# A softmax attention on one core: row maxima in steps of eight tiles, scores 14 tiles behind, outputs gathered by SBUF transfers instead of transposes

## The chip, the cores and the metric

The kernel runs on one core of a Trainium2 chip. The metric is the device time of one execution in microseconds (us), the median over runs. Engines in the text: PE (TensorE), DVE (VectorE), ACT (ScalarE), POOL (GpSimd), and SP (SyncE), which here only issues transfers.

## The reference

The program is four layers on 2 x 1024 tokens of width 128: a delta-rule attention, a mixture of experts (two of eight), a softmax attention with rotary positions, and a second mixture of experts (one of eight). Only the third layer changes:

```python
x = layernorm(h)
q, k, v = x @ Wq.T + bq, x @ Wk.T + bk, x @ Wv.T + bv     # 16 heads of 8, 2 sequences of 1024
q, k = rope(q), rope(k)
p = softmax(q @ k.T / sqrt(8))                              # 1024 x 1024 for each head and sequence
h = h + (p @ v) @ Wo.T + bo                                 # then the layernorm of the next layer
```

## The kernel before

**Precision by rows.** A head has only 8 dimensions, so q and k are split into three bf16 parts and the products of parts are laid on 56 rows (`KR`) of the contraction. The parts are stored to DRAM by `store`, and loaded again in that layout by `load`, `load_q` and `group`. There are two copies: one on partitions 64 to 119 (`S1B`), for the maxima, and one on partitions 0 to 58 (`KA`), whose three extra rows carry the negated row maximum in three bf16 parts, so that the second product already is the score minus its maximum.

**Stages.** Four heads of one sequence make a group; there are eight (`G`). The work on them is one long pipeline:

- A *tile* is 128 queries of one head against all 1024 keys: two matmuls of 512 columns (`max_half`) into a pair of PSUM banks, and one DVE `tensor_reduce` (`max_tile`, L1063) to a column of maxima. There are 256 tiles, and two pairs of banks take turns.
- After every 16 tiles (512 queries of four heads), POOL negates and splits the 16 columns (`split_rows`), PE turns them into rows (`turn_rows`, L950), ACT copies the rows to SBUF (`rows`, L1192), and SP sends them to the extra rows of q (`max_rows`, L1347). A counter `e` numbers these rounds.
- A *unit* is one block of 128 keys against 512 queries for four heads: four score matmuls (`scores`, L961) into banks that rotate by three, four exponentials of 128x512 on ACT (L1201), and four fp32 matmuls with the values (`values`, L974), two units later, which add up in bank 7. There are 128 units, and eight of them complete 512 queries. A column of ones beside the values gives the sum of the exponentials. ACT copies bank 7 to `a1_o` (L1214).
- PE's order is written out by hand: 22 tiles (`AHEAD`) first, then in each unit two tiles and the four scores, half and half, with the values of two units before. The last 11 units have no tiles beside them. The first unit of each eight waits for the row transfer (`a1_mrow`).

**After the last tile** DVE takes the 16 outputs one by one (`turn`): a 32x32-block transpose of 128x512 (L1086), a reciprocal of the sums (L1090) and a product (L1091), and after each four a transpose back (`turn_back`, L1096). PE then multiplies by Wo (`project_out`, L983); the first two of these four stand in PE's order inside the last units. DVE adds the result to x (`add_out`, L1101) and takes the statistics of the next layernorm (L118, L121).

**SP's order** is also written out by hand. Its queue first stores q and k, then loads groups as buffers come free. In the first rounds loads, stores and row transfers alternate; from round 3 on, every second round also issues the two loads of a later group.

Of the kernel before, what the change touches and what calls it, by code (L numbers as in the profile page):

```python
# [12 lines left out]
P = 128  # L13
# [10 lines left out]
AHEAD_AT = TABLES_AT - 12376 - 3076  # L24
# [775 lines left out]
AHEAD = 22  # L800
# [6 lines left out]
OUT_UNITS = {G * U - 7: 0, G * U - 5: 1}  # L807
# [5 lines left out]
def evictions():  # L813


    out = [("rows", 0)]
    for n in range(G * U * HG):
        out.append(("score", n))
        if n % HG == 1 and n // HG % NTB == NTB - 2 and n // HG + 2 < G * U:
            out.append(("rows", (n // HG + 2) // NTB))  # L820
    return out
# [16 lines left out]
def attn1_memory(c, w):  # L838
    c.sb("a1_part", [P, 4, 3, BLK], BF16)
    c.sb("a1_v", [P, NT, D])  # L840
    c.sb("a1_q", [P, NG, QH, HG, BLK], BF16)
# [3 lines left out]
    c.sb("a1_mx", [P, 2, HG * 4])  # L845
    c.sb("a1_mn", [P, 2, HG * 4])
    c.sb("a1_mt", [P, P], BF16)
    c.sb("a1_ob", [P, 2, BLK])
    c.sb("a1_rd", [P, 2, BLK // 32])
# [3 lines left out]
def attn1_ahead(c):  # L853

    pool, at = c.pool, AHEAD_AT
    for name, shape, dtype in (("a1_k", [P, NG, HG, L], BF16), ("a1_va", [P, NTB, NH, 32], F32), ("a1_ms", [P, 3, HG * 4], BF16), ("a1_id", [P, P], BF16)):
        c.mem[name] = c.arena.cut(at, shape, dtype)
        at += words_of(shape, dtype)
# [3 lines left out]
    pool_step(c, pool.memset(c.mem["a1_va"][:, :, :, HD:HD + 1], 1.0))  # L862
# [3 lines left out]
def attn1_loads(c, w):  # L866

    at = TABLES_AT - 3076
    c.ahead = Count(c.nc, "ahead")
    for name, shape, whole in (("wq", [D, D], False), ("wqs", [D, D], False), ("wk", [D, D], False), ("wks", [D, D], False),  # L870
                               ("wv", [D, D], False), ("wo", [D, D], False), ("bcol", [D, 4], False), ("bv", [P, D], True),
                               ("bo", [P, D], True), ("cos", [D, L], False), ("sin", [D, L], False)):
# [7 lines left out]
def tile_at(n):  # L880

    return n // 32, n % 32 // 16, n % 16 // 4, n % 4
# [7 lines left out]
def attn1_pe(c):  # L890
# [25 lines left out]
    def max_half(n, half):  # L916
        g, qh, h, qt = tile_at(n)
        k, bank = g % NG, 3 + 2 * (n % 2)
        if half == 0:
# [5 lines left out]
            if n == 16:  # L925
                pe.wait_ge(S("a1_second"), 16)
            if n >= 32 and n % 32 == 0:
                pe.wait_ge(S(f"a1_one{g}"), 3 * 16)
# [3 lines left out]
        mm = pe.matmul(ps[:, bank + half, :], q[rows, k, qh, h, qt * P:(qt + 1) * P],  # L932
# [10 lines left out]
    def turn_rows(e):  # L943
# [6 lines left out]
        pe.matmul(ps[0:3 * HG * 4, bank_of(i), 0:P], m["a1_ms"][:].rearrange("p i a -> p (i a)"), m["a1_id"][:],  # L950
                  start=True, stop=True).then_inc(S("a1_s2"), 1)

    def scores(u, h):
        st, qh, kb = u // U, u % U // NTB, u % NTB
        k, i = st % NG, TAKEN["score", u * HG + h]
        if h == 0 and u % U == 0:
            pe.wait_ge(S(f"a1_two{st}"), 3 * 16)
        if h == 0 and kb == 0:
            pe.wait_ge(S(f"a1_mrow{qh}"), 16 * (st + 1))
# [4 lines left out]
    def values(u, half=None):  # L964
        st, qh, kb = u // U, u % U // NTB, u % NTB
        at = slice(0, BLK) if half is None else slice(half * (BLK // 2), (half + 1) * (BLK // 2))
        if half != 1:
            if kb == 0:
                pe.wait_ge(S("a1_va"), st + 1)
                if u >= NTB:  # L970
                    pe.wait_ge(S("a1_o"), u // NTB)
            pe.wait_ge(S("a1_exp"), TAKEN["score", u * HG + HG - 1] + 1)
        for h in range(HG):
            mm = pe.matmul(ps[32 * h:32 * h + 32, 7, at], va[:, kb, (st % NG) * HG + h, :],  # L974
                           pt[:, (u % 3) * HG + h, at], start=kb == 0 and half != 1, stop=kb == NTB - 1, skip_group_check=True)
        if half != 0:
            mm.then_inc(S("a1_pv"), 1)

    def project_out(b):
        pe.wait_ge(S("a1_back"), b + 1)  # L980
        pe.wait_ge(S("a1_exp"), max((i + 1 for i in range(FIVE, len(TAKEN)) if bank_of(i) == 3 + b), default=1))
        for j in range(TPB):
# [1662 lines left out]
```

## Time and profile before

| | |
|---|---|
| median of 3 runs | 858.94 us (858.55 to 862.6) |
| profiled execution | 860.77 us, of which the span is 859.0 us |
| TensorE's granted clock, mean over the span | 0.903 |
| busy over the whole span | PE 715.8, DVE 658.8, ACT 526.6, POOL 238.3 us |
| the changed layer | about 399 to 762 us of the span |

Times in the views are microseconds from the span's start; "x" counts instructions. A name after an arrow in brackets is what an idle engine waited for. `arena` is the one big SBUF allocation, so most tiles have this name. SPq rows are transfers being issued.

### The profile page before, as it was taken

The page shows a single profiled execution, that of the slowest core. Times are in us where ns is not written, and L with a number is a line of the kernel's source. Part 1 is how long each engine was busy: PE and PEld are TensorE (multiplying, and loading weights), DVE is VectorE, ACT ScalarE, POOL GpSimd, SP SyncE. Part 2 cuts the span into 40 slices and gives each one's busy share as a digit, 9 for nine tenths or more (in the row PEclk, how much of TensorE's full clock was granted, in tenths as well). Part 3 has the DMA queues.
Part 4 walks back from the last instruction along what each step waited for, and adds up shares of the span by engine and source line. Part 5 has one row for each costly group of instructions (what it writes and reads, how often), then busy time and mean ns, then how long its engine had stood idle before and what let it go on. Part 6 is the DMA issues. An engine that isn't in the chain of part 4 may idle for free. (4 is left out here: it accounts for less than half of the span.)

```text
span 859.0 us, 20505 instructions
## 1 busy us (share of the span) xinstructions
PE 715.8 (83%) x8024; PEld 359.3 (42%) x8024; DVE 658.8 (77%) x1317; ACT 526.6 (61%) x1028; POOL 238.3 (28%) x295
## 2 busy tenths in 40 slices
PE   5999978887736999963989999999999999946880
PEld 2333236553426999961412222222222222236770
DVE  7887985446875555537799999999999999664555
ACT  3763622365713444425629999999999999624453
POOL 0130010204216767552473300100000100006773
PEclk9999989997856999985958999999999999767995
DMA  3440010000082311221756650403300000032123
GB/s 101 98 100 3 1 24 5 4 3 1 0 302 95 110 48 50 38 61 60 205 129 148 170 126 2 88 16 75 73 16 2 2 2 9 4 128 84 50 50 101
DMA packets 40968, 55.47 MB, mean 65 GB/s; under 512 B 9210, under 2 KB 31234, under 8 KB 40490
## 3 DMA queue, kind: packets, MB, share of 16 engines
q1 hardware_dynamic: 36906, 46.04, 20.1%
q0 software_dynamic: 3968, 8.13, 3.5%
q8 instruction: 64, 1.05, 0.5%
q14 instruction: 30, 0.25, 0.1%
HBM read 35.22 MB, written 14.55 MB: 58 GB/s over the span
## 5 line engine op out<-in xcount | busy, mean ns | idle before, releaser
L1063 DVE TENSOR_REDUCE arena<-psum 128x1 f32<-128x1024 f32 x256 | 292.8, 1217 | 10.4 <-PE psum L932 10.4
L1201 ACT ACTIVATE arena<-psum 128x512 f32<-128x512 f32 x512 | 276.5, 597 | 18.7 <-PE psum L961 11.4
L932 PE MATMUL psum<-arena 56*128 56x512 bf16 x512 | 164.5, 404 | 4.7 <-DVE arena L1063 3.6
L974 PE MATMUL psum<-arena 128*32 128x256 f32 (+1 forms) x1944 | 163.4, 408 | 5.9 <-issue 5.9
L961 PE MATMUL psum<-arena 59*128 59x512 bf16 x512 | 158.4, 390 | 0.1
L369 PE MATMUL psum<-arena 128*128 128x128 f32 x808 | 108.1, 281 | 0.4 <-DVE arena L420 0.4
L369 PEld LDWEIGHTS psum<-arena 128*128 128x128 f32 x808 | 102.0, 198 | 0.7 <-DVE arena L420 0.7
L974 PEld LDWEIGHTS psum<-arena 128*32 128x32 f32 x1944 | 38.8, 108 | 107.5 <-issue 61.6
L932 PEld LDWEIGHTS psum<-arena 56*128 56x128 bf16 x512 | 28.9, 95 | 115.6 <-DVE arena L1063 97.9
L485 POOL DMA_INDIRECT rows_y<-arena x62 | 62.6, 1009 | 37.7 <-DVE arena L434 31.9
L396 PE MATMUL psum<-arena 128*128 (+1 forms) x496 | 66.5, 277 | 2.8 <-ACT arena L464 2.0
L480 POOL DMA_INDIRECT arena<-rows_x,arena x62 | 60.0, 968 | 26.0 <-issue 17.4
L1273 POOL TENSOR_SCALAR arena<-arena 128x16 f32<-128x16 f32 x16 | 4.1, 254 | 220.4 <-DVE arena L1063 220.3
L396 PEld LDWEIGHTS psum<-arena 128*128 128x128 f32 x496 | 60.3, 192 | 4.8 <-issue 3.3
L461 ACT ACTIVATE arena<-psum 128x512 f32<-128x512 f32 x39 | 23.3, 597 | 44.1 <-PE psum L369 44.1
L453 ACT COPY arena<-arena 128x512 f32 x39 | 24.1, 618 | 32.0 <-PE psum L369 19.4
L2300 PE MATMUL psum<-arena 128*32 128x512 f32 x352 | 41.2, 593 | 0.2 <-DMA arena<-arena 0.2
L424 DVE TENSOR_TENSOR arena<-arena,psum 128x512 f32<-128x512 f32 x39 | 26.8, 687 | 18.4 <-PE psum L369 18.4
L961 PEld LDWEIGHTS psum<-arena 59*128 59x128 bf16 x512 | 30.6, 94 | 17.3 <-ACT arena L1201 14.2
L434 DVE COPY arena<-psum 128x128 f32<-128x128 f32 x62 | 18.1, 292 | 25.0 <-PE psum L396 13.5
L2040 ACT ACTIVATE arena<-psum 128x64 f32<-128x64 f32 x32 | 7.2, 225 | 44.7 <-PE psum L2322 44.7
L417 DVE COPY arena<-arena 128x512 f32 x39 | 17.0, 437 | 19.2 <-issue 16.2
(314 smaller groups left out, 1059.5 us busy)
## 6 DMA issues: line engine op xcount, KB each, us to landing
arena<-scr_q SPq DMA_DIRECT2D x32, 224.0 KB
arena<-scr_k SPq DMA_DIRECT2D x15, 448.0 KB
arena<-in_f_up SPq DMA_DIRECT2D x1, 4096.0 KB, 14.0
arena<-rows_y SPq DMA_DIRECT2D x12, 256.0 KB, 4.8
scr_q<-arena SPq DMA_DIRECT2D x6, 384.0 KB, 5.3
arena<-in_f_down SPq DMA_DIRECT2D x1, 2048.0 KB, 17.0
arena<-in_f_up SPq DMA_DIRECT2D x1, 2048.0 KB, 9.4
rows_x<-xn SPq DMA_DIRECT2D x5, 256.0 KB, 13.0
```

Of the source, the lines that this page charges most:

```text
L369: mm = pe.matmul(ps[:, bank, f * P:(f + 1) * P], w[:, a.pair, at], xt[:, a.pair, :], start=True, stop=True)
L396: mm = pe.matmul(ps[:, 5 + 2 * d.pair, 0:P], h[:, d.pair, f * P:(f + 1) * P], merged(wdown[:, ed, f * P:(f + 1) * P]), start=f == 0, stop= ...
L424: dve.tensor_tensor(h[:, u.pair, :], sg[:, u.pair, :], ps[:, 2 + u.pair, :], ALU.mult).then_inc(hidden, 1)
L453: act.copy(m["e_w"][:, x0.pair, F:2 * F], merged(m["e_up"][:, bass.ds(e, 1), F:2 * F])).then_inc(picked2, 1)
L480: pool.indirect_dma_start(xs[:, t % GATHERED, :], None, src, index).then_inc(landed[t % GATHERED], 16)
L485: pool.indirect_dma_start(dst, index, y[:, d.slot, :], None).then_inc(stored[d.slot], 16)
L932: mm = pe.matmul(ps[:, bank + half, :], q[rows, k, qh, h, qt * P:(qt + 1) * P], kk[rows, k, h, half * BLK:(half + 1) * BLK], start=True, s ...
L961: pe.matmul(ps[:, bank_of(i), :], kk[0:KA, k, h, kb * P:(kb + 1) * P], q[0:KA, k, qh, h, :], start=True, stop=True).then_inc(S("a1_s2"), 1)
L974: mm = pe.matmul(ps[32 * h:32 * h + 32, 7, at], va[:, kb, (st % NG) * HG + h, :], pt[:, (u % 3) * HG + h, at], start=kb == 0 and half != 1 ...
L1063: dve.tensor_reduce(mx[:, qh, h * 4 + qt:h * 4 + qt + 1], ps[:, bank:bank + 2, :].rearrange("p a b -> p (a b)"), X, ALU.max).then_inc(S("a ...
L1201: act.activation(pt[:, (u % 3) * HG + h, :], ps[:, bank_of(i), :], ACT.Exp, scale=float(HD) ** -0.5).then_inc(S("a1_exp"), 1)
L2300: mm = pe.matmul(ps[32 * h:32 * h + 32, fir_bank(n, i), :], m["a0_wfir"][:, (g0 + g) * H0 + h, :], v4[:, h, b, PAD + t0 - 4 * g:PAD + t0 - ...
```

## The change

- The row maxima go on in rounds of 8 tiles (`TE`), that is 256 queries (`QW`) of four heads. There are 32 rounds (`QE`) of split, turn, copy and row transfer in place of 16.
- PE runs 14 tiles ahead of the scores, not 22. The last 7 units have no tiles beside them.
- A unit is two key blocks against 256 queries. Its four score banks each hold two heads, so a score of 512 columns becomes two matmuls of 256. The values add up in the first half of bank 7, over four units, and ACT's copy of the output is 128x256, 32 times. The loads of q are cut into four of 256 queries.
- The ones beside the values fill eight columns, so that each head's sum of exponentials comes out on eight rows. SP gathers the rows of each output into one dense array in `xnT`, and the replicated sums into `xn`: eight transfers of 8 rows x 256 for each of 30 outputs (`collect`). The last two outputs are gathered by two small matmuls with a 0/1 matrix (`pick`).
- DVE's 16 transposes, reciprocals and products and its four transposes back are gone. In their place there are reciprocals of 128x256 and products of 128x256 (`divide`, `divide_last`).

The core of the diff (from layout, memory and loads only the lines that the text speaks of):

```diff
-AHEAD = 22
+QW, TE, UE = 256, 8, 4
+QE = TILES // TE
+AHEAD = 14
-OUT_UNITS = {G * U - 7: 0, G * U - 5: 1}
+OUT_UNITS = {G * U - 6: 0, G * U - 5: 1, G * U - 3: 2}
...
         free_bank(i)
-        pe.matmul(ps[:, bank_of(i), :], kk[0:KA, k, h, kb * P:(kb + 1) * P],
-                  q[0:KA, k, qh, h, :], start=True, stop=True).then_inc(S("a1_s2"), 1)
+        for x in range(2):
+            h = 2 * (j % 2) + x
+            mm = pe.matmul(ps[:, bank_of(i), x * QW:(x + 1) * QW], kk[0:KA, k, h, kb * P:(kb + 1) * P],
+                           q[0:KA, k, e % 4, h, :], start=True, stop=True)
+        mm.then_inc(S("a1_s2"), 1)
...
+    def divide(n):
+        at = slice(n * QW, (n + 1) * QW)
+        of = slice(0, P if n < 6 else 96)
+        dve.wait_ge(S(f"a1_dense{n}"), (NG if n < 6 else NG - 1) * 2 * HG * 16)
+        dve_step(c, dve.reciprocal(sums[of, at], sums[of, at]))
+        z = dve.tensor_tensor(dense[of, at], dense[of, at], sums[of, at], ALU.mult)
...
-    for n in range(2 * NG):
-        turn(n)
-    turn_back(0)
-    turn_back(1)
...
+    for n in range(4):
+        divide(n)
+    add_out(0)
+    add_out(1)
+    divide(4)
+    divide(5)
     add_out(2)
...
+    def collect(e):
+        g, n = e // 4 % NG, e // 16 * 4 + e % 4
+        at = slice(n * QW, (n + 1) * QW)
+        part = o[:, e // 2, e % 2 * QW:(e % 2 + 1) * QW]
+        sp.wait_ge(S("a1_o"), e + 1)
+        for h in range(HG):
+            to = slice((g * HG + h) * HD, (g * HG + h + 1) * HD)
+            sp.dma_start(dense[to, at], part[32 * h:32 * h + HD, :]).then_inc(S(f"a1_dense{n}"), 16)
+            sp.dma_start(sums[to, at], part[32 * h + HD:32 * h + 2 * HD, :]).then_inc(S(f"a1_dense{n}"), 16)
...
     group(0, 0, "a1_two0")
     group(S1B, 1, "a1_one1")
+    store_all(4)
     max_rows(0)
...
+    for e in (5, 6):
+        max_rows(e)
+    for e in range(4):
+        collect(e)
     store_all(7)
-    for e in range(3, 2 * G):
+    for e in range(7, QE):
+        collect(e - 3)
         max_rows(e)
-        if e % 2 == 1 and e // 2 + 3 < G:
-            g = e // 2 + 3
+        if e % 4 == 3 and e // 4 + 3 < G:
+            g = e // 4 + 3
```

How rows of the program move, at three places. First SP, where the first maxima are sent. Before, from the load of the second half of the first q on; the rows named scr_q and scr_k are loads or stores of q and k, and L1347 is the row transfer of round 0:

```order
L1332 DMA arena<-scr_q 56x4x512
L1332 DMA arena<-scr_k 56x4x1024
L1332 DMA arena<-scr_q 56x4x512 x2
L1332 DMA arena<-scr_k 56x4x1024
L1332 DMA arena<-scr_q 56x4x512 x2
L1347 DMA arena<-arena 3x16x128
```

After the change, at the same place (L1349 is the load, L1342 the store, L1363 the row transfer):

```order
L1349 DMA arena<-scr_q 56x4x256 x2
L1349 DMA arena<-scr_k 56x4x1024
L1349 DMA arena<-scr_q 56x4x256 x4
L1349 DMA arena<-scr_k 56x4x1024
L1349 DMA arena<-scr_q 56x4x256 x4
L1342 DMA scr_k<-arena 128x3x512
L1342 DMA scr_k<-arena 128x2x512 x2
L1363 DMA arena<-arena 3x8x128
```

Ahead of the first row transfer there now stand twelve loads in place of seven, and three stores that stood behind it.

Second SP, ahead of the row transfer of round 7 of the changed kernel. It is preceded by the transfers of rounds 5 and 6 (one row, "x2"), then 32 gathering transfers (16 times the pair L1372, L1373), and then:

```order
L1342 DMA scr_q<-arena 128x3x512 x2
L1342 DMA scr_q<-arena 128x512
L1372 DMA xnT<-arena 8x256
L1373 DMA xn<-arena 8x256
L1372 DMA xnT<-arena 8x256
L1373 DMA xn<-arena 8x256
L1372 DMA xnT<-arena 8x256
L1373 DMA xn<-arena 8x256
L1372 DMA xnT<-arena 8x256
L1373 DMA xn<-arena 8x256
L1363 DMA arena<-arena 3x8x128
```

Before, between one row transfer and the next, SP had at this depth of the program (from round 2 to round 3):

```order
L1347 DMA arena<-arena 3x16x128
L1332 DMA arena<-scr_k 56x4x1024
L1332 DMA arena<-scr_q 56x4x512 x2
L1325 DMA scr_q<-arena 128x3x512 x2
L1325 DMA scr_q<-arena 128x512
L1325 DMA scr_q<-arena 128x3x512 x2
L1325 DMA scr_q<-arena 128x512
L1347 DMA arena<-arena 3x16x128
```

So 43 transfers stand between the row transfers of rounds 6 and 7, where no more than nine stood between two of them before.

Third DVE, behind the last `tensor_reduce`. Before, from the tiles to the first of the 16 outputs:

```order
L1063 TENSOR_REDUCE arena<-psum 128x1 x256
L1086 STREAM_TRANSPOSE arena<-arena 128x512
L1090 RECIPROCAL arena<-arena 128x16
L1091 TENSOR_TENSOR xn<-arena 128x16x8
L1086 STREAM_TRANSPOSE arena<-arena 128x512
```

After the change:

```order
L1101 RECIPROCAL xn<-xn 128x256
L1102 TENSOR_TENSOR xnT<-xnT,xn 128x256
L1115 TENSOR_TENSOR x<-x,psum 128x512
L118 BN_STATS bn<-x 128x6 x4
L121 BN_AGGR mv<-bn 128x2 x4
L1115 TENSOR_TENSOR x<-x,psum 128x512
```

The reciprocal is now of 256 elements on each partition, where it was of 16, and it comes ten times in all (four of them in a row before the first `add_out`), where it came 16 times.

## Rows read from the trace of the kernel before

**Rows 1.** The page, busy time of each engine over the span

```profile
PE 715.8 (83%) x8024; PEld 359.3 (42%) x8024; DVE 658.8 (77%) x1317; ACT 526.6 (61%) x1028; POOL 238.3 (28%) x295
```

**Rows 2.** Busy time by stretch: engines, granted clock, share of the DMA engines, GB/s

```profile
428.00:442.00 14.00, 12.31 (x24) 1.49 (x24) 14.00 (x13) 2.47 (x4) 10.15 (x11) 0.50 0.69 148
...
446.00:461.00 15.00, 13.96 (x92) 2.94 (x90) 14.22 (x13) 11.46 (x23) 4.85 (x5) 0.66 0.77 185
461.00:465.00 4.00, 4.00 (x45) 1.10 (x41) 4.00 (x4) 3.94 (x9) 2.41 (x7) 1.00 0.01 2
560.00:590.00 30.00, 29.24 (x317) 7.29 (x313) 29.62 (x27) 29.18 (x57) 1.09 (x5) 1.00 0.32 63
732.80:743.00 10.20, 10.20 (x40) 2.91 (x37) 9.68 (x30) 5.08 (x10) 0.00 (x0) 0.50 0.00 0
```

**Rows 3.** Timeline: start, length, instruction, idle before; rounds of 16 tiles, exponentials alone

```profile
702.11 0.25 POOL L1273 TENSOR_SCALAR arena<-arena 128x16 f32<-128x16 f32 x1 [17.02 <-DVE arena L1063]
704.71 0.25 ACT L1192 CAST arena<-psum 48x128 bf16<-48x128 f32 x1
712.70 0.59 ACT L1214 COPY arena<-psum 128x512 f32<-128x512 f32 x1
720.51 0.25 POOL L1273 TENSOR_SCALAR arena<-arena 128x16 f32<-128x16 f32 x1 [17.02 <-DVE arena L1063]
744.44 6.48 ACT L1201 ACTIVATE arena<-psum 128x512 f32<-128x512 f32 x13
```

**Rows 4.** Timeline of the start: first tiles, loads of two groups, first score

```profile
423.18 22.37 DVE L1063 TENSOR_REDUCE arena<-psum 128x1 f32<-128x1024 f32 x19 [6.01 <-PE psum L932]
428.69 0.35 SPq L1332 DMA_DIRECT2D arena<-scr_k  x1
448.54 0.58 PE L961 MATMUL psum<-arena 59*128 59x512 bf16 x1
449.05 2.36 SPq L1325 DMA_DIRECT2D scr_k<-arena  x3
```

**Rows 5.** SP's issues by line: duration ns min/median/max, first and last start

```profile
L1332 SPq DMA_DIRECT2D arena<-scr_q x32: 307/419/2028, 417.3 to 616.9; - x32
L1347 SPq DMA_DIRECT2D arena<-arena x16: 697/716/863, 445.3 to 723.7; - x16
L1576 SPq DMA_DIRECT2D arena<-arena x32: 507/592/894, 29.9 to 52.2; - x32
```

**Rows 6.** Timeline and stretches: a row transfer waited for; loads of two groups

```profile
723.66 0.70 SPq L1347 DMA_DIRECT2D arena<-arena  x1
725.84 0.11 PEld L961 LDWEIGHTS psum<-arena 59*128 59x128 bf16 x2 [0.61 <-DMA arena<-arena]
540.07 0.46 SPq L1332 DMA_DIRECT2D arena<-scr_k  x1
552.00:554.00 2.00, 2.00 (x26) 0.54 (x24) 2.00 (x3) 1.96 (x5) 0.00 (x0) 1.00 0.04 8
```

**Rows 7.** DVE's groups by shape over the span: busy, mean ns

```profile
L1775 DVE TENSOR_TENSOR xn<-arena 128x256 f32<-128x256 f32 x4 | 1.6, 428 | 0.0
...
L1858 DVE RECIPROCAL arena<-arena 128x32 f32<-128x32 f32 x2 | 0.7, 354 | 0.1
L1090 DVE RECIPROCAL arena<-arena 128x16 f32<-128x16 f32 x16 | 4.1, 254 | 0.6
```

**Rows 8.** Timeline of the end: a wait of PE, the add and statistics, next layer

```profile
731.05 1.16 PE L983 MATMUL psum<-arena,xnT 128*128 128x128 f32 x8 [1.11 <-DVE xnT L1096]
752.23 0.69 DVE L1101 TENSOR_TENSOR x<-x,psum 128x512 f32<-128x512 f32 x1 [7.46 <-PE psum L983]
752.95 0.87 DVE L118 BATCH_NORM_STATS2 bn<-x 128x6 f32<-128x128 f32 x4
753.86 0.38 DVE L121 BATCH_NORM_AGGREGATE mv<-bn 128x2 f32<-128x6 f32 x4
761.75 0.19 DVE L668 TENSOR_SCALAR rs<-mv 128x4 f32<-128x4 f32 x1 [1.26 <-PEq L2621]
```

More of the change, by code:

```diff
@@ L818, in evictions @@
         out.append(("score", n))
-        if n % HG == 1 and n // HG % NTB == NTB - 2 and n // HG + 2 < G * U:
-            out.append(("rows", (n // HG + 2) // NTB))
+        if n % HG == 1 and n // HG % UE == UE - 2 and n // HG + 2 < G * U:
+            out.append(("rows", (n // HG + 2) // UE))
     return out
@@ L931, in max_half @@
         rows = slice(S1B, S1B + KR)
-        mm = pe.matmul(ps[:, bank + half, :], q[rows, k, qh, h, qt * P:(qt + 1) * P],
+        mm = pe.matmul(ps[:, bank + half, :], q[rows, k, qq, h, qt * P:(qt + 1) * P],
                        kk[rows, k, h, half * BLK:(half + 1) * BLK], start=True, stop=True)
@@ L964, in values, with scores @@
[L964 to L972, printed above, removed]
+    def scores(u, j):
+        st, e, kb = u // U, u // UE, 2 * (u % UE) + j // 2
+        k, i = st % NG, TAKEN["score", u * HG + j]
+        if j == 0 and u % U == 0:
+            pe.wait_ge(S(f"a1_two{st}"), 5 * 16)
+        if j == 0 and u % UE == 0:
+            pe.wait_ge(S(f"a1_mrow{e % 2}"), 16 * (e // 2 + 1))
+        free_bank(i)
+        for x in range(2):
[3 more added lines that the diff above has]
+        mm.then_inc(S("a1_s2"), 1)
@@ L973, in values @@
+    def values(u, i):
+        st, e, kb = u // U, u // UE, 2 * (u % UE) + i
+        if kb == 0:
+            pe.wait_ge(S("a1_va"), st + 1)
+            if e:
+                pe.wait_ge(S("a1_o"), e)
+        pe.wait_ge(S("a1_exp"), TAKEN["score", u * HG + 2 * i + 1] + 1)
         for h in range(HG):
-            mm = pe.matmul(ps[32 * h:32 * h + 32, 7, at], va[:, kb, (st % NG) * HG + h, :],
-                           pt[:, (u % 3) * HG + h, at], start=kb == 0 and half != 1, stop=kb == NTB - 1, skip_group_check=True)
@@ L987, in attn1_pe, with project_out @@
+    def project_out(b, halves=range(2)):
+        if b >= 2:
+            pe.wait_ge(S("a1_added"), b - 1)
+        for n in halves:
+            pe.wait_ge(S("a1_back"), 2 * b + n + 1)
+            for j in (2 * n, 2 * n + 1):
+                mm = pe.matmul(ps[:, 3 + b % 2, j * D:(j + 1) * D], xnT[:, (b * TPB + j) * P:(b * TPB + j + 1) * P],
+                               m["a1_wo"][:], start=True, stop=True)
+        if halves[-1] == 1:
+            mm.then_inc(S("a1_out"), 1)
     project(0)
@@ L1117, in attn1_dve @@
     dve.tensor_scalar(rs[:, most], mv[:, most, 1], 1e-5, None, ALU.add).then_inc(S("a1_nvar"), 1)
-    turn(halves - 1)
-    turn_back(3)
+    divide(6)
+    divide(7)
     dve.wait_ge(S("a1_nroot"), 1)
@@ L1182, in attn1_act @@
     biased(7)
-    for n in (4, 5):
-        leading(n)
-        following(n)
+    leading(4)
+    following(4)
     def rows(e):
@@ L1418, in attn1_layout @@
     out["a1_wv"] = a["L1_attn_Wv"].T
-    out["a1_wo"] = a["L1_attn_Wo"].T.reshape(NG, HG, HD, D).transpose(1, 0, 2, 3).reshape(D, D)
+    out["a1_wo"] = a["L1_attn_Wo"].T
+    pick = np.zeros((HG, 32, 2, HG, HD), np.float32)
+    for h in range(HG):
+        for d in range(HD):
+            pick[h, d, 0, h, d] = pick[h, HD, 1, h, d] = 1
+    out["a1_sel"] = pick.reshape(P, 64)
     bq, bk = a["L1_attn_bq"], a["L1_attn_bk"]
```

217 lines of the change are left out of this document (106 added, 111 removed).

## The prediction

> **What bounds the kernel now.** I read the page first: no engine is busy all the time, since the program is four layers [rows 1]. Only the third changes, so I went on by stretches. From 560 to 590 us, in the middle of the pipeline, DVE is busy 29.62 of 30 us and reduces 27 tiles, one in 1.107 us; ACT is busy 29.18 us [rows 2]. DVE sets the pace, and ACT is close behind. The timeline gives the round: the same POOL instruction comes at 702.11 and at 720.51 [rows 3], 18.40 us for 16 tiles. That is 1.150 us a tile and 2.30 us a unit. 16 x 1.107 would be 17.71, so 0.69 us a round is lost around the row copy of 0.25 us and the output copy of 0.59 us on ACT [rows 3]. Exponentials alone go at 6.48 / 13 = 0.50 us each, a unit at 2.0 us [rows 3].
>
> The start: tiles begin at 423.18 us and go at 22.37 / 19 = 1.177 us each, at half the clock [rows 2, 4]; the first score starts at 448.54, after 22 tiles [rows 4]. The end: the last tile is reduced by 720.4 (this is when POOL starts its last round, and the outputs begin), and the next layer starts at 761.75 [rows 8]. So the tail behind the last tile is 41.4 us. In it PE waits 1.11 us for DVE at 731.05 [rows 8], and from 732.8 to 743 it runs at the lower clock, 0.50 [rows 2].
>
> The total is thus the start of the tiles, plus 256 tiles at DVE's pace, plus every stall of DVE among them, plus the tail. Running 14 tiles ahead and not 22 doesn't shorten the row of 256 tiles; it leaves 7 units behind it and not 11, which pays only if the tail was bound by these units.
>
> **The first score (+6.5, bounds 0 and +8.5).** With 14 tiles ahead DVE runs dry at 423.2 + 14 x 1.177 = 439.7 unless the scores have begun. They wait for the row transfer of round 0. Before, it had an empty queue. Now twelve loads and three stores stand ahead of it. Three sets of this size (two groups of loads, one set of stores) were issued from 446 us on, the stores last, at 449.05 [rows 4], and the DMA engines were done by 461, at most 15 us after [rows 2]. From 428.7, when the first load is issued [rows 4], that gives about 443.5; the q loads, cut in pieces half as long, may add 1. The row transfer lands right behind, about 445.5, and DVE goes on at 446.2: a stall of 6.5 us. Low bound: small transfers get past the big ones. Then SP's issues alone count: 12 x 0.46, three stores 2.4, the transfer's own 2.16 us from issue to landing (723.66 to 725.82, where the weight load at 725.84 waited for it [rows 6]). That is before 439.7, and costs nothing. High bound: the loads slow each other by 2 us more.
>
> **The 43 transfers ahead of round 7 (+11, bounds +6 and +19).** A round now is 4 units, 9.2 us. The row copy falls in the middle of the third unit, and the scores that need the transfer come 1.5 units (3.45 us) behind the turn on PE, which with the copy of 0.25 us on ACT [rows 3] and the hand-over takes 0.5: about 3.0 us behind SP's start. So between two row transfers SP has 9.2 us, and 0.8 of slack (3.0 less 2.16). Between rounds 6 and 7 it must issue 40 gathering transfers and three stores. What one costs: loads 0.42 at the median and 0.31 at least; transfers from SBUF to SBUF 0.59 with 32 rows, 0.70 with the row transfer [rows 5]; 0.04 us lie between two. For 8 rows I take 0.40 + 0.04, near the loads, since it has fewer rows than either SBUF transfer. 40 x 0.44 = 17.6, the stores 2.4, the row transfer's own issue 0.7: 20.7, against 10.0 allowed. Stall 10.7. With 0.31 + 0.02 it is 6, with 0.59 + 0.04 it is 18.5. PE executes in order, so the tiles queued behind that score wait too, DVE has at most two tiles in its banks, and ACT nothing.
>
> The Trainium skill, "DMA: Bandwidth & Descriptors", section "Anatomy of one DMA — SWDGE (gpsimd) path", puts the sequencer's dispatch at about 50 ns. At that price 40 transfers would be 2 us, and this stall would not exist; the rows of SP's queue show six to fourteen times as much, and the sum goes by them.
>
> **Rounds with group loads (+6, bounds 0 and +12).** Four rounds (7, 11, 15, 19) issue ten loads behind the row transfer, and then eight gathering transfers stand ahead of the next one. Issue: 0.7 + 10 x 0.46 + about 0.8 for one slow one (the maximum is 2.0 [rows 5]) + 3.5 = 9.6 us, just over 9.2. Worse, the data: two groups issued from 540.07 keep the DMA engines busy until 552 [rows 6], 12 us; with half-length pieces 12.5 to 13. A row transfer issued at +9.6 lands behind them at about +13.7, and it is due at 9.2 + 3.0 = 12.2. That is 1.5 us a round, four rounds. Low bound: nothing, if it overtakes. High bound: 3 us each. Before, 18.4 us lay between two row transfers, so this was hidden.
>
> **Clock (+3, bounds 0 and +8).** Behind the 1.11 us wait at 731.05 the granted clock was at its lower level (1.2 GHz of 2.4) for 10.2 us, and ACT did 10 exponentials in them [rows 2], 1.0 us each and not 0.5. A stall of 11 us will do the same. I take 2 us for the long one and 1 for the others; part of the low stretch lies in the stalls.
>
> **Per round (+3.5, bounds 0 and +11).** The losses of 0.69 come from one row copy and one output copy. Now there are two of each in the same time, with the output copy half as wide (about 0.35). I take 0.9 in place of 0.69, 16 times. If the loss does not shrink with the copy it is 16 x 0.69 = 11. ACT stays under DVE: 16 x 0.50 + 0.25 + 0.35 = 8.6 against 8 x 1.107 = 8.86 us.
>
> **The tail (-5.5, bounds -19 and 0).** DVE's reciprocals: 16 elements 254 ns, 32 elements 354 ns [rows 7]. That is 6.25 ns an element, so 256 elements take 1.75 us. With the product of 0.43 [rows 7] and the gap a `divide` is 2.25 us. An `add_out` is 0.69 + 0.87 + 0.38 [rows 8] and gaps, 2.05. From the last tile: four divides 9.0, two add_outs 13.1, two divides 17.6; PE waits for these two before it projects (0.7) and `add_out(2)` ends at 20.5. Two divides of 96 partitions 25.0 (time goes by elements on a partition), small ones 25.6, `divide_last` 27.8, four rows of norm 29.0, `divide_last` 31.2, PE 0.7, the last `add_out` 34.0, and 1.3 to the next layer (the gap ahead of 761.75 [rows 8]): 35.3. With 0.6 for waits, 35.9 against 41.4. PE and ACT need only 7 units (14 us) and three projections in this time, so DVE is the bound. If a reciprocal took one cycle an element (0.43 us, like the product), ten would be 13.2 shorter and PE the bound: about 22.5 us, -19. The other end is 0: waits of PE and the lower clock eat the gain.
>
> The Trainium skill, "VectorE: DVE Perf Modes", section "First, the fixed hardware budget", says that a reciprocal iterates with a repeat count of 8. With the page's 0.96 GHz that is an estimate of 2.1 us for 256 elements, and the tail would be 3.8 us longer than by the rows.
>
> **At nothing:** POOL's split (five instructions, under 1.5 us, due 2.2 us later as before), the wider memset (hidden in the layer before), the table loads of the next layer (SP has them out long before 35 us of tail have passed).
>
> **Sum:** 6.5 + 11 + 6 + 3 + 3.5 - 5.5 = +24.5 us, on the profiled execution's 860.8: 885.3. That execution is 1.8 above the median of the runs, so I predict 883.
>
> **Rivals.**
> - *Only the long stall.* Row transfers overtake the group loads, so the rounds with loads cost nothing, and the first score comes on time: 858.9 + 11 + 2 + 3.5 - 5.5 = 870. For it: no row shows a small transfer behind a big one. Against: the loads of one queue finish one after the other. 18 in 100.
> - *Short reciprocals.* The tail takes -19 in place of -5.5: 870. Against: the two shapes above give a slope of six cycles. 10 in 100.
> - *Weight loads bind PE.* Each score now takes two weight loads where it took one, and the values in the tail twice as many. In the steady stretch PE is modelled busy 29.24 of 30 us [rows 2]. If 0.06 us of each of the 512 extra loads shows, +30 more: 910. Against: DVE's reduce, not PE, is back to back, and most of a load hides behind the matmul before. 7 in 100.
> - *SP's queue is never late* (the other side). If a gathering transfer issues in at most (10.0 - 0.7 - 2.4) / 40 = 0.17 us and small transfers land past big ones, all waits are gone, the clock stays up, and the tail gain is kept: 858.9 + 3.5 - 5.5 = 857, and 853 if the rounds lose nothing more. It decides at 0.17 us; no issue of these lines is under 0.307 [rows 5]. 7 in 100. The dispatch figure of the Trainium skill named above is the rule by which it would come out this way.
> - The forecast: 58 in 100, its own range 871 to 900.
>
> **From the cases to the numbers.** About 0.5% is what a measurement here can tell from no change, 4.3 us. The queue rival splits: 4 faster, 3 the same. Some of the 870 cases, with a start at its low bound, end within 0.5%: 3. So faster 0.05, the same 0.06, slower 0.89. To leave out no more than 2 in 10, the range runs from 865 to 905: the bottom takes in the two cases of 870, the top the long issue (0.63 each, +8) with the high bound of the load rounds.
>
> **What would show each step.** SP's issues of the gathering lines at about 0.4 us; PE's score waiting some 11 us for the row transfer at about 510 us of the span, with a gap in DVE's reduces; shorter waits 9 us later and then each 37 us, three times; the first score at about 445 with DVE idle before it; reciprocals of 128x256 at 1.75 us; about 36 us from the last reduce to the next layer. The prediction is wrong if SP's issues are below 0.2 us, if row transfers land 2.2 us after issue while group loads run, or if PE's period with split scores is above DVE's.

## The result and the profile after

The changed kernel takes 903.49 us (median of 4 runs, 899.7 to 904.37) against 858.75 us before (856.66 to 862.6), a ratio of 1.0507 with a 95% interval of 1.0459 to 1.0555. That is 44.7 us more, where 24.5 were forecast: inside the range of 865 to 905 us, in the direction, and too little by nearly half. The profiled execution took 903.59 us, its span 902.3.

The page of the changed kernel: busy time of each engine, and two of its costliest groups (busy, mean ns | idle just before them and what ended it):

```profile
PE 728.8 (81%) x8664; PEld 411.3 (46%) x8664; DVE 663.7 (74%) x1285; ACT 528.1 (59%) x1061; POOL 253.1 (28%) x375
...
L1082 DVE TENSOR_REDUCE arena<-psum 128x1 f32<-128x1024 f32 x256 | 298.0, 1217 | 48.7 <-PE psum L932 46.6
...
L963 PE MATMUL psum<-arena 59*128 59x256 bf16 x1024 | 168.4, 283 | 31.2 <-DMA arena<-arena 23.5
```

DVE's busy sum moves by 4.9 us [rows 1], so the loss isn't work. The reduces sat idle for 48.7 us, and PE's scores waited 23.5 of theirs for a row transfer. Where the idle time lies is read from the timeline of the reduces (start, length, count, idle before):

```profile
422.39 16.49 DVE L1082 TENSOR_REDUCE arena<-psum 128x1 f32<-128x1024 f32 x14 [6.01 <-PE psum L932]
443.64 5.99 DVE L1082 TENSOR_REDUCE arena<-psum 128x1 f32<-128x1024 f32 x5 [4.76 <-PE psum L932]
...
488.79 22.32 DVE L1082 TENSOR_REDUCE arena<-psum 128x1 f32<-128x1024 f32 x19 [0.24 <-PE psum L932]
530.27 1.23 DVE L1082 TENSOR_REDUCE arena<-psum 128x1 f32<-128x1024 f32 x1 [19.16 <-PE psum L932]
532.63 1.22 DVE L1082 TENSOR_REDUCE arena<-psum 128x1 f32<-128x1024 f32 x1 [1.14 <-PE psum L932]
534.39 7.12 DVE L1082 TENSOR_REDUCE arena<-psum 128x1 f32<-128x1024 f32 x6 [0.53 <-PE psum L932]
542.93 2.51 DVE L1082 TENSOR_REDUCE arena<-psum 128x1 f32<-128x1024 f32 x2 [1.42 <-PE psum L932]
...
583.70 2.51 DVE L1082 TENSOR_REDUCE arena<-psum 128x1 f32<-128x1024 f32 x2 [1.82 <-PE psum L932]
...
625.16 1.22 DVE L1082 TENSOR_REDUCE arena<-psum 128x1 f32<-128x1024 f32 x1 [2.60 <-PE psum L932]
...
666.21 1.22 DVE L1082 TENSOR_REDUCE arena<-psum 128x1 f32<-128x1024 f32 x1 [2.08 <-PE psum L932]
...
669.90 93.26 DVE L1082 TENSOR_REDUCE arena<-psum 128x1 f32<-128x1024 f32 x80 [0.82 <-PE psum L932]
```

The first gap is behind exactly 14 tiles. The big one, 19.16 us, is at round 7. Then come four groups of gaps about 41 us apart, each with two or three small gaps behind the first. These lie in stretches of the lower clock: the granted clock is 0.51 from 585 to 588 us, and 0.50 from 668 to 670. The last 80 tiles run without a gap. In SP's queue ahead of the big gap (first and last rows of the 43 transfers):

```profile
498.00 0.70 SPq L1363 DMA_DIRECT2D arena<-arena  x1
498.75 0.71 SPq L1372 DMA_DIRECT2D xnT<-arena  x1
...
519.93 0.62 SPq L1373 DMA_DIRECT2D xn<-arena  x1
520.60 1.56 SPq L1342 DMA_DIRECT2D scr_q<-arena  x3
522.21 0.67 SPq L1372 DMA_DIRECT2D xnT<-arena  x1
...
527.59 0.77 SPq L1363 DMA_DIRECT2D arena<-arena  x1
...
538.59 0.77 SPq L1363 DMA_DIRECT2D arena<-arena  x1
```

From the row transfer of round 6 to that of round 7 SP needs 29.6 us. Forty gathers take 0.667 each, 26.7 us, three stores 1.6. And PE's first score of round 7 starts 2.0 us behind the issue:

```profile
529.59 0.39 PE L963 MATMUL psum<-arena 59*128 59x256 bf16 x1 [18.87 <-DMA arena<-arena]
```

By stretch (PE, weight loads, DVE, ACT and POOL busy, granted clock, DMA share, GB/s), the big gap, what follows it, the steady part and the tail:

```profile
512.00:529.00 17.00, 0.00 (x0) 0.00 (x0) 0.00 (x0) 0.00 (x0) 0.00 (x0) 0.54 0.20 65
529.00:540.00 11.00, 10.24 (x104) 3.97 (x104) 8.00 (x7) 7.82 (x16) 1.01 (x5) 0.78 0.91 173
...
700.00:760.00 60.00, 58.83 (x732) 23.87 (x729) 59.62 (x53) 57.76 (x118) 6.49 (x31) 1.00 0.04 10
763.00:806.00 43.00, 31.68 (x249) 15.73 (x248) 30.50 (x65) 22.41 (x46) 1.11 (x6) 0.81 0.08 26
```

In the big gap no engine works, and the DMA engines are busy a fifth of the time: the kernel waits for SP to issue, not for bandwidth. The tail takes from the last reduce (763.16) to 805.94, 42.8 us. DVE in it:

```profile
763.08 1.74 DVE L1101 RECIPROCAL xn<-xn 128x256 f32<-128x256 f32 x1
764.86 0.42 DVE L1102 TENSOR_TENSOR xnT<-xnT,xn 128x256 f32<-128x256 f32 x1
...
781.00 0.69 DVE L1115 TENSOR_TENSOR x<-x,psum 128x512 f32<-128x512 f32 x1 [1.31 <-PE psum L998]
...
794.06 0.23 DVE L1133 RECIPROCAL rs<-rs 128x12 f32<-128x12 f32 x1 [6.62 <-ACT rs L1230]
...
799.97 1.76 DVE L1109 RECIPROCAL xn<-psum 32x256 f32<-32x256 f32 x1 [2.08 <-PE psum L989]
...
805.94 0.19 DVE L668 TENSOR_SCALAR rs<-mv 128x4 f32<-128x4 f32 x1 [0.87 <-PEq L2662]
```

The divides cost what was forecast, but DVE waits 6.62 us for a root on ACT. ACT takes it behind the last exponentials, and these are late because PE, which goes through its list in order, first stood before the third projection:

```profile
779.74 1.22 PE L998 MATMUL psum<-arena,xnT 128*128 128x128 f32 x4 [1.35 <-DVE xnT L1102]
780.89 1.03 PE L963 MATMUL psum<-arena 59*128 59x256 bf16 x4
```

Its next scores take 1.03 us and no longer 0.61: the granted clock is 0.50 from 780 to 789. Between the last exponentials, which end at 788.5, and the root ACT has two things more, and both are part of DVE's wait: the copy of the last output, which waits 3.50 us for PE's last products with the values, and the load of the table for the root.

```profile
792.04 0.37 ACT L1208 COPY arena<-psum 128x256 f32<-128x256 f32 x1 [3.50 <-PE psum L975]
792.43 1.28 ACT L165 ACT_TABLE_LOAD   x1
...
793.83 0.20 ACT L1230 ACTIVATE rs<-rs 128x12 f32<-128x12 f32 x1
```

Where the 43.3 us between the spans are (859.0 and 902.3), against the forecast's own terms.

| | forecast | measured | from |
|---|---|---|---|
| start | 6.5 | 4.4 | gaps of the reduces to round 6, 6.7 us, less 2.3 before |
| ahead of round 7 | 11, and 2 of clock | 20.8 | gaps of the reduces, 19.16 + 1.14 + 0.53 |
| rounds with group loads | 6, and 1 of clock | 13.1 | their gaps: 2.7, 3.1, 4.0, 3.3 |
| pace, rest | 3.5 | 5.3 | 340.8 us from first to last tile, less 297.2 before, less the three rows above |
| tail | -5.5 | +1.4 | 42.8 less 41.4 |

The other layers add -0.8 and -0.9 us, which no run explains.

### The profile page after: what moved, and what is told of

Same layout as the page of the kernel before. It is cut to its first block and busy times, and to the rows that moved or that the text cites. A ratio compares the mean times of both kernels' runs of the same rounds, so it can differ in the third digit from the quotient of the medians.

```text
span 902.3 us, 22268 instructions
## 1 busy us (share of the span) xinstructions
PE 728.8 (81%) x8664; PEld 411.3 (46%) x8664; DVE 663.7 (74%) x1285; ACT 528.1 (59%) x1061; POOL 253.1 (28%) x375
## 5 line engine op out<-in xcount | busy, mean ns | idle before, releaser
L1082 DVE TENSOR_REDUCE arena<-psum 128x1 f32<-128x1024 f32 x256 | 298.0, 1217 | 48.7 <-PE psum L932 46.6
L963 PE MATMUL psum<-arena 59*128 59x256 bf16 x1024 | 168.4, 283 | 31.2 <-DMA arena<-arena 23.5
L975 PE MATMUL psum<-arena 128*32 128x256 f32 x2048 | 170.9, 406 | 5.1 <-issue 5.1
L963 PEld LDWEIGHTS psum<-arena 59*128 59x128 bf16 x1024 | 76.2, 96 | 56.9 <-DMA arena<-arena 19.2
L1284 POOL TENSOR_SCALAR arena<-arena 128x8 f32<-128x8 f32 x32 | 7.4, 232 | 248.4 <-DVE arena L1082 242.0
L975 PEld LDWEIGHTS psum<-arena 128*32 128x32 f32 x2048 | 42.6, 110 | 63.7 <-ACT arena L1217 34.8
L2081 ACT ACTIVATE arena<-psum 128x64 f32<-128x64 f32 x32 | 7.2, 225 | 42.2 <-PE psum L2363 42.1
```

What stands on the lines that cost most here:

```text
L963: mm = pe.matmul(ps[:, bank_of(i), x * QW:(x + 1) * QW], kk[0:KA, k, h, kb * P:(kb + 1) * P], q[0:KA, k, e % 4, h, :], start=True, stop=True)
L975: mm = pe.matmul(ps[32 * h:32 * h + 32, 7, 0:QW], va[:, kb, (st % NG) * HG + h, :], pt[:, (u % 3) * HG + 2 * i + h // 2, h % 2 * QW:(h % 2 ...
L1082: dve.tensor_reduce(mx[:, e % 4, n % TE:n % TE + 1], ps[:, bank:bank + 2, :].rearrange("p a b -> p (a b)"), X, ALU.max).then_inc(S("a1_red ...
```

## The experiments

The twelve runs below were made on three chips. The kernel before takes 886.79 us on the first (spread, none, the rounds with group loads, the start), 855.16 on the second (the changed kernel again, pairs, the third projection, the four edits together) and 858.34 on the third (22 tiles ahead, no reciprocals, gathers of four rounds, divides on POOL). So runs on different chips are compared by their ratio to the kernel before, and microseconds are subtracted only on one chip or between traces. The changed kernel itself was measured in the result above and on the second chip; for the other two its ratio is taken to be the same, 1.0507 to 1.0535. The changed kernel on the second chip:

**The changed kernel again.** 

> The changed kernel as it is, as the reference of the other runs on the same chip. Both theories: the ratio to the kernel before stays near 1.05 (1.043 to 1.057), whatever the chip's own level, and the long gap of DVE ahead of round 7's scores is 19 us again.

900.65 us, ratio 1.0535 (1.0498 to 1.0572); the long gap is 19.17 us, and the tail 42.2 us (the last reduce ends at 761.08, the next layer starts at 803.31). The interval overlaps that of the result, so no effect of the chip on the lost share can be told.

### The 240 gathering transfers

**Spread.**
```diff
+    later = [(e, heads) for e in range(QE - 2) for heads in ((0, 1), (2, 3))]
     for e in range(7, QE):
-        collect(e - 3)
         max_rows(e)
...
+        for _ in range(1 if e % 4 == 3 and e < 20 else 3):
+            if later and later[0][0] <= e - 2:
+                collect(*later.pop(0))
```


> Edit: the same 240 gathering transfers, but each row transfer is issued first and the gathers are spread behind it, six to twelve... at most twelve a round (four behind a round that loads groups), so that SP's issues fit into a round. Queue theory (SP's issue time of 0.67 us for each of 40 gathers is the 19 us stall ahead of round 7): that stall goes, with the half-clock units behind it, 20 us less, 884 us; the waits in the rounds with group loads stay if they are the data's, and shrink by up to 1 us each if they are SP's. Rival (the stall is the landing of stores and gathers in the DMA engines, not their issue): the same bytes flow in the same stretch, so the stall would move behind another round and the time stay above 895.

Ratio 1.0193 (1.0116 to 1.027), 3.1 to 3.4 points of the ratio, some 27 to 29 us, under the changed kernel. The same 240 transfers, none ahead of round 7. That is more than the 20 us expected: the long gap is gone and has moved nowhere else, and the gaps of the load rounds shrink from 13.1 to 5.8 us in all, since the row transfer is now ahead of the gathers. Reduces from the middle of round 4 on:

```profile
503.99 31.61 DVE L1082 TENSOR_REDUCE arena<-psum 128x1 f32<-128x1024 f32 x27 [0.24 <-PE psum L932]
537.12 37.46 DVE L1082 TENSOR_REDUCE arena<-psum 128x1 f32<-128x1024 f32 x32 [1.53 <-PE psum L932]
575.79 37.46 DVE L1082 TENSOR_REDUCE arena<-psum 128x1 f32<-128x1024 f32 x32 [1.21 <-PE psum L932]
```

**None.** `collect` issues nothing, and the divides wait for the outputs alone.


> Leaves out all 240 gathering transfers (the output is not the attention's). Prices them all. Queue theory: the long stall is gone and SP is free in every round; what stays are the waits behind the data of two groups. 882 us, within 3 us of the kernel with spread gathers. If gathers also cost elsewhere (SBUF ports, DMA engines), it is more than 5 us below that kernel.

Ratio 1.014 (1.0067 to 1.0213), 4.2 us under the spread version on the same chip. Reduces from the middle of round 4 on:

```profile
502.89 69.18 DVE L1082 TENSOR_REDUCE arena<-psum 128x1 f32<-128x1024 f32 x59 [0.24 <-PE psum L932]
572.52 37.46 DVE L1082 TENSOR_REDUCE arena<-psum 128x1 f32<-128x1024 f32 x32 [0.45 <-PE psum L932]
610.84 37.46 DVE L1082 TENSOR_REDUCE arena<-psum 128x1 f32<-128x1024 f32 x32 [0.86 <-PE psum L932]
648.47 95.44 DVE L1082 TENSOR_REDUCE arena<-psum 128x1 f32<-128x1024 f32 x82 [0.18 <-PE psum L932]
```

At the first load round no gap is left that makes a row of its own, and at the others 0.45, 0.86 and 0.18 us: with the gathers away, ten loads are hardly felt. I had expected the waits behind the loads' data to stay. All gathers together cost 32 to 34 us (3.7 to 4.0 points), of which their order alone gives back 27 to 29.

**Pairs.** One transfer for two rounds (the divides wait for it):
```diff
-        part = o[:, e // 2, e % 2 * QW:(e % 2 + 1) * QW]
+        if e % 2 == 0:
+            return
+        n, at = n - 1, slice((n - 1) * QW, (n + 1) * QW)
+        part = o[:, e // 2, :]
```


> The gathering transfers carry two rounds at once, 8 rows of 512 columns, so 120 of them take the place of 240 and move the same bytes. Theory A (a transfer holds SP's queue for a time of its own, 0.62 us, whatever its size): 20 transfers of 13.3 us with gaps stand ahead of round 7 in place of 26.7, the long gap of DVE falls from 19.2 us to about 6, and the kernel is 12 to 16 us faster than the changed one. Theory B (issue time goes by bytes): each issues in 1.1 us or more, the gap stays at 17 to 21 us and the time is within 3 us.

886.45 us, ratio 1.0381 (1.0329 to 1.0433), 14.2 us under the changed kernel on the same chip. SP's issues of it, with twice the bytes each (line: duration ns min/median/max, first and last start):

```profile
L1374 SPq DMA_DIRECT2D xnT<-arena x60: 624/624/712, 499.5 to 755.8; - x60
```

The changed kernel's own row has the same minimum and a median one nanosecond longer:

```profile
L1372 SPq DMA_DIRECT2D xnT<-arena x120: 624/625/878, 498.8 to 771.2; - x120
```

The bytes have no part in the price. The long gap falls to 3.12 us:

```profile
515.03 1.23 DVE L1082 TENSOR_REDUCE arena<-psum 128x1 f32<-128x1024 f32 x1 [3.12 <-PE psum L932]
```

My 6 counted 20 transfers; it is 16, since the fifth round has no partner yet: 16 x 0.667 + 1.6 + 0.7 = 13.0 us, less the 10.0 that the forecast allowed, is 3.0.

### The rounds with group loads

```diff
             group(S1B, g, f"a1_one{g}")
-            sp.wait_ge(S("a1_pv"), U * (g - NG + 1))
-            group(0, g, f"a1_two{g}")
+        if e % 4 == 1 and 8 < e < 22:
+            g = e // 4 + 2
+            sp.wait_ge(S("a1_pv"), U * (g - NG + 1))
+            group(0, g, f"a1_two{g}")
```


> Edit: of the two group loads that four rounds issue together, the second is issued two rounds later. The waits behind them were 13 us in all in the changed kernel (DVE idle in rounds 8, 12, 16, 20 with the half clock after it). Data theory (the row transfer lands behind 1.8 MB of loads): with half of it ahead, 5 us of data against 9.2 us of round, all four go: 903.5 - 13 = 890 or 891. Rival (SP's issue is late by itself, 0.8 + 5.3 + 5.3 us of issues against 9.2): with five loads fewer it also fits, but round 7's neighbour, round 8, stays late, since SP is still behind there: 894. A third view, that small transfers pass big ones, gives no change.

Ratio 1.0381 (1.0306 to 1.0455), 1.3 points or 11 us under the 1.0507 of the changed kernel, with intervals that just don't meet. Past round 7 the timeline has one row for 184 tiles:

```profile
550.30 213.69 DVE L1082 TENSOR_REDUCE arena<-psum 128x1 f32<-128x1024 f32 x184 [0.60 <-PE psum L932]
```

All four waits are gone, and only they. With this run and the one without gathers, neither the loads nor the gathers alone make these waits: both stand between two row transfers. In the changed kernel the row transfer behind the first such round was issued at 538.59, 11.0 us after the one before (9.6 forecast), and the first score behind it started at 542.5, 3.9 us later and not 2.0. In the other three such rounds the row transfer comes 11.5 to 11.9 us after the one before, and the score 2.9 to 3.4 us behind it. So it is issued late and it also lands late.

### The start

```diff
     group(0, 0, "a1_two0")
-    group(S1B, 1, "a1_one1")
-    store_all(4)
     max_rows(0)
+    group(S1B, 1, "a1_one1")
+    store_all(4)
```


> Edit: the row transfer of round 0 is issued ahead of the second group's loads and the three stores. DVE stood idle 4.8 us behind tile 14 and 1.4 us soon after. Theory (the first row transfer lands behind loads and stores): it lands at about 438, before DVE is through with 14 tiles; 903.5 - 6 = 897.5. Rival (the first group's own data is what the first score waits for, not the rows): that lands only 2 us earlier, 901 or more.

Ratio 1.0443 (1.0364 to 1.0521); the interval holds the changed kernel's 1.0507, so here the timeline decides. The first row has 19 tiles without a gap, where it had 14, and the gaps up to round 6 add up to 2.94 us in place of 6.65, 3.7 less where 6 were expected:

```profile
437.50 22.42 DVE L1082 TENSOR_REDUCE arena<-psum 128x1 f32<-128x1024 f32 x19 [6.01 <-PE psum L932]
```

**22 tiles ahead.** `AHEAD = 22`, all else as changed.


> The changed kernel with 22 tiles ahead in place of 14, all else as it is. Theory A: the start gap of 5 us goes, since tiles last until 449; the long gap of 19 us stays, since the turn of a round's rows stands at a fixed place in PE's order; in the tail eleven units follow the last tile, 24 us by themselves, but PE then finds the divides done and waits for none, so the tail stays at 41 to 43 us. Sum 4 to 7 us less than the changed kernel, ratio to before 1.045 to 1.049. Theory B (the shorter lead is worth its four units): tail 8 us longer, the time 2 to 4 us more than the changed kernel.

903.11 us, ratio 1.0543 (1.05 to 1.0585): no measurable difference from 14. The start gap is gone (27 tiles in the first row), the long gap stays at 19.14 us, and the tail is 46.5 us (758.31 to 804.82), 4.3 longer than in the changed kernel again. The number lies between the two theories: I had the tail unchanged, as PE's waits would pay for four more units. PE then waits only 1.24 us for a divide and keeps its clock, but the four units more weigh more than that.

### The tail

**Third projection later.**
```diff
-OUT_UNITS = {G * U - 6: 0, G * U - 5: 1, G * U - 3: 2}
+OUT_UNITS = {G * U - 6: 0, G * U - 5: 1}
...
+    project_out(2)
     values(G * U - 2, 0)
```


> The third projection of outputs is moved in PE's order from inside the last units to behind the last scores; nothing is left out. Theory A (the tail's gain is lost because this projection, which waits for DVE's sixth divide, stands ahead of two units' scores, so that the last exponentials, the root on ACT and the gathering matmuls come late, at half clock): no idle time of PE ahead of it, DVE's wait for the root falls from 6.6 us to under 1, and from the last reduce to the next layer it takes 36 to 37 us in place of 42.8, so 6 us less than the changed kernel, ratio to it 0.993. Theory B (ACT's own work behind the last exponentials, the table load of 1.3 us among it, bounds the tail): under 2 us less.

897.46 us, ratio 1.051 (1.0468 to 1.0552), 3.2 us under the changed kernel, within what a measurement can't tell; the profile tells it. DVE's root row comes with no wait:

```profile
786.09 0.22 DVE L1134 RECIPROCAL rs<-rs 128x12 f32<-128x12 f32 x1
```

and the tail is 38.8 us (760.26 to 799.05), 3.4 less. The mechanism holds, the 6 us not: DVE now waits 2.97 us for the third projection itself, and the waits for the small matmuls (2.08 us) and around the last projection stay.

**No reciprocals.** Each is a `tensor_copy` of the same shape.


> Left out: the reciprocals of the sums in the tail (ten of 256 elements); a plain copy of the same shape stands in their place, so the outputs aren't normalised. Theory A (DVE's divides are what PE's last projections wait for, and these waits delay the last exponentials): a copy takes 0.3 to 0.45 us in place of 1.75, PE's waits of 0.7 to 1.4 us ahead of the first three projections go, the last two units run at the full clock, and from the last reduce to the next layer it takes 29 to 33 us in place of 42.3; 10 to 13 us less than the changed kernel, ratio to before 1.038 to 1.042. Theory B (the chain behind the last exponentials bounds the tail by itself): under 4 us less.

892.06 us, ratio 1.0419 (1.0373 to 1.0465), 0.9 to 1.2 points or 8 to 10 us under the changed kernel. What it computes is not normalised. A copy takes 0.26 to 0.43 us; the tail is 33.2 us (760.13 to 793.37), 9.0 less for 14 us less DVE work (ten by some 1.4). So the reciprocals were binding, but 5 us of them lay beside PE's and ACT's chain: even without them, and with the granted clock at 1.00 to the last scores, DVE waits 5.5 us for ACT's root.

```profile
783.07 0.23 DVE L1133 RECIPROCAL rs<-rs 128x12 f32<-128x12 f32 x1 [5.52 <-ACT rs L1230]
```

### All together

**Four edits** (spread gathers, second load later, first rows first, third projection later).


> Four edits together: gathering transfers in halves, spread and behind the row transfer; the second group load two rounds later; the first row transfer ahead of the second group's loads; the third projection behind the last scores. Nothing is left out. If the gains add (-28, -11, -5.7 and -6 us of those seen or expected for each alone, of 44.6 lost), it ends at the kernel before or 2 to 6 us under it: ratio 0.992 to 1.003. Rival: the loads and gathers moved out of one place collide in another, as the rounds then have little slack, or the steady pace (0.016 us a tile more) is worse: ratio 1.005 to 1.015.

866.41 us, ratio 1.0156 (1.0108 to 1.0204): next to the rival's 1.005 to 1.015. 34 of the 45 us come back, where the gains by ratio of the single edits add to 48 (28, 11, 5.7, 3.2; of the 5.7 the timeline shows 3.7). Seven of these were counted twice: spreading the gathers had by itself cut the gaps of the load rounds from 13.1 to 5.8 us, which the later loads were then credited with again. Another 4.2 stay as gaps of 1.00, 0.70, 1.26 and 1.24 us at the load rounds, and 4.1 in gaps of the start. From first to last tile it takes 307.8 us where 297.2 were needed before.

**Gathers of four rounds at once,** with the other three edits (64 gathers, of which only the first eight still stand ahead of the row transfer of round 7; the divides wait for them by fours):
```diff
-        part = o[:, e // 2, e % 2 * QW:(e % 2 + 1) * QW]
+        rounds = 4 if e % 4 == 3 else 2
+        first = e - rounds + 1
+        part = o[:, first // 2:first // 2 + rounds // 2, :].rearrange("p a t -> p (a t)")
```


> As the kernel with all four edits, but gathers of four rounds at once in place of spread halves, and no work moved to POOL: the control for the one before. Nothing is left out. Expected: no gap of DVE over 2 us in the pipeline, the tail 37 us, ratio to before 1.005 to 1.014, 1 to 6 us less than with spread gathers. If the gain over the spread gathers is nothing, the number of transfers no longer matters once none is late.

860.3 us, ratio 1.003 (1.0005 to 1.0054), 1.3 points under the spread version, which was measured on another chip. The traces show 7.0 us less from first to last tile (300.8) and 0.7 more in the tail. Expected were 1.005 to 1.014. From the middle of round 4 on all tiles are one row:

```profile
482.22 238.18 DVE L1083 TENSOR_REDUCE arena<-psum 128x1 f32<-128x1024 f32 x205 [0.24 <-PE psum L932]
```

So the number of gathers still mattered. What remains against the kernel before is the pace, 238.18 / 205 = 1.162 us a tile against 18.40 / 16 = 1.150 (round to round [rows 3]), 3.0 us on 256 tiles, while the tail gives 3.6 back (37.8 against 41.4). So the change is worth nothing here even with its waits cured, and no version beat the kernel before.

**Four divides moved to POOL** (the same gathers, the loads and first rows as above, the third projection as in the changed kernel; a power of -1 and a product on POOL in rounds 21 to 24).


> Nothing is left out. The gathers take four rounds at once (64 transfers of 1024 or 512 columns in place of 240), behind the row transfer of a round; second group load two rounds later; first row transfer ahead of the second group's loads; the first four divides are made by POOL, as a power of -1 and a product, between its splits of rounds 21 to 24, and DVE does only two divides ahead of the first projections. If a transfer costs 0.62 to 0.67 us whatever its size, eight of them stand ahead of round 7 and no long gap is left; DVE's tail falls by four divides, 8.5 us, and PE's third projection waits for nothing: 25 to 32 us from the last reduce to the next layer. Against the kernel before: steady pace +4, gaps +4, tail -9 to -16: 1 to 8 us less, ratio 0.990 to 0.999. Rival: a power on POOL takes longer than the 9.2 us of a round and stalls its splits, or four rows of gathers at once collide with group loads: ratio 1.005 or more.

1005.38 us, ratio 1.1729 (1.169 to 1.1769): a plain failure, by the rival. POOL's rows:

```profile
632.54 0.31 POOL L1300 MEMSET arena<- 128x256 f32 x1
632.93 41.28 POOL L1301 TENSOR_TENSOR xn<-xn,arena 128x256 f32<-128x256 f32 x1
674.28 0.72 POOL L1302 TENSOR_TENSOR xnT<-xnT,xn 128x256 f32<-128x256 f32 x1
```

A power takes 41.3 us where the product behind it takes 0.72. POOL's next split waits, with it the row transfer, the scores and DVE: four gaps of 32.7 to 33.9 us. This run doesn't compute the attention, so it gives a price and no version. One cause stands in its edit: the exponent -1 is written to `a1_t`, and that is the same memory as the second half of `a1_o`. The `memset` at 632.54 overwrites the output of round 16, copied there at 604.86, before SP gathers it from 677.71 on. So how exact the values of the power are is not shown. Moving four divides off DVE in another way wasn't tried.

## Why the prediction came out as it did

**Right about SP's queue but short in size, and wrong about the tail.** The waits lie where the prediction put them. Two of its steps failed. The first is the price of a gather, "for 8 rows I take 0.40 + 0.04, near the loads": it measured 0.667 us. The second is the step in the tail, "PE and ACT need only 7 units (14 us) and three projections in this time, so DVE is the bound": there the engines wait for each other. Of the 18.8 us between forecast and measured spans, 7.8 are ahead of round 7, 6.1 in the rounds with group loads, 6.9 in the tail and 1.8 in the pace; the start takes 2.1 back and the other layers 1.7. That the time stayed inside the range owes something to luck: the top allowed for the long issue and for slower load rounds, and both came, but for no tail longer than before.

- *Transfers ahead of round 7.* A gather is 0.667 us from issue to issue (0.624 and a gap), and 40 take 26.7 us, not 17.6. My high bound of 0.63 was the nearest, and it came from the right row: the SBUF-to-SBUF transfers of 0.59 and 0.70 [rows 5]. I argued that fewer rows cost less. Rows of 1, 2 and 4 KB all take 0.624 at the median (the changed kernel at 0.625, pairs, fours), so the bytes don't set the price. That the kind of transfer does is what the rows suggest (SBUF to SBUF 0.59 to 0.76, loads 0.42); a load of 8 rows wasn't run. The stores, taken at 2.4 us, took 1.6. With 0.667 the same sum gives 26.7 + 1.6 + 0.7 - 10.0 = 19.0, against 19.16 measured. The low clock behind it cost the 1.7 us of the two small gaps, close to the 2 taken. The Trainium skill, "DMA: Bandwidth & Descriptors", section "Anatomy of one DMA — SWDGE (gpsimd) path", gives some 50 ns of sequencer dispatch for a transfer issued from GpSimd. These transfers are issued from SP, so the figure isn't theirs; SP's rows show twelve times as much, and no run here tests the GpSimd path.
- *Group loads.* The same price again: eight gathers are 5.3 and not 3.5 us, which is the 1.4 us by which the next row transfer was later than forecast, and more. I had counted issue as just short and the data as the cause; the run without gathers shows that loads alone cost under 1 us a round. 13.1 us in place of 7.
- *Start.* 4.4 for 6.5. The row transfer was issued at 436.05, and the score behind it started at 442.99, 6.9 us later and not 2.0: it was held up behind the loads and stores, and came 2.5 us earlier than the 445.5 forecast.
- *Pace.* 5.3 for 3.5, inside its bounds. In the steady part a round of eight tiles comes every 9.29 us, which is (9.29 / 8 - 1.150) x 256 = 2.9 us; the rest lies outside it. The working behind it misread the rows: 29.62 / 27 is 1.097 and not 1.107, and the 27 tiles include those cut by the ends of the stretch. From start to start in the trace a tile takes 1.131 us in both kernels. So a round of 16 lost 0.30 us and not 0.69, and 16 tiles of the changed kernel lose 0.48 and not 0.9. The difference of the two guesses, 0.21, came near the true 0.18.
- *Tail.* +1.4 for -5.5, outside its bounds of -19 and 0. The reciprocal was right (1.72 to 1.76 us for 1.75 forecast); the estimate of 2.1 us from the Trainium skill, "VectorE: DVE Perf Modes", section "First, the fixed hardware budget", is too long by a fifth. The step that failed is that I summed each engine by itself. DVE's sixth divide holds PE, which is in order, PE holds the last exponentials and, behind them, ACT's last output copy, then come the table load of 1.28 us and the root, and the root holds DVE. Two runs bear this out, with 3.4 us for the order of one projection and 9.0 for the reciprocals; what the copy and the table load are worth wasn't tested. The 0.6 us "for waits" should have been 8 to 9 (6.62 + 2.08).

Of the rivals, *SP's queue is never late* fell with the price, and *only the long stall* with the waits of rounds 8, 12, 16 and 20. *Weight loads bind PE* at 30 us would have shown as a pace of 1.27 us a tile; it is 1.161. *Short reciprocals* would have saved 9 us, not the 13.5 that I gave it.

What stays open is why the pace lost its 0.011 us a tile; no run tested it. In the steady part of the trace each round of eight has two long steps, 1.235 and 1.255 us in place of 1.131, next to ACT's output copy (0.38 us) and its row copy (0.25 us), and there are twice as many of these copies as before.

## What to carry to other kernels

Count the transfers that a queue must issue between two that something waits for, price each by the nearest transfer of the same kind (from DRAM, or SBUF to SBUF), and compare with the time between the two. If it doesn't fit, put the transfer that is waited for first (27 to 29 us here), and make fewer and longer transfers (14 us here for half their number). In a tail where engines hand over to each other in program order, walk the hand-overs one after the other: a sum for each engine alone gives a bound and not a time.

## What the hardware showed that I hadn't expected

- A gather from SBUF to SBUF of 8 rows occupies SP's queue for 0.624 us, with 1, 2 or 4 KB a row, while a load of 56 partitions takes 0.42 at the median [rows 5].
- In the stretch of 17 us in which no engine worked the DMA engines were busy 0.20 of the time: here SP's queue of small transfers held up a machine that was otherwise idle.
- A power on POOL costs 41.3 us for 128x256 elements, 161 ns for each of the 256 on a partition, against 0.72 us for a product of the same shape.
- A reciprocal on DVE takes the same 1.72 to 1.76 us for 256 elements, from SBUF on 128 or 96 partitions and from PSUM on 32; a plain copy from PSUM takes 0.43 and from SBUF 0.26 to 0.29.
